# Retention: VectorE's routing work of an earlier group goes ahead of the residual and the keys

## The reference

```
x = x + attn(cond(x))                       # retention, 16 heads of 8
  attn: y = ((q k^T) * decay / sqrt(8)) v;  y = (y - mean) / sqrt(var + eps) per head
        return (y * gn_weight + gn_bias) @ W_o.T
x = x + ffn(cond2(x))
  cond2: gate = softmax(rmsnorm(x) @ wg_W + wg_b + cond_256 @ gg_W + gg_b)
         topk_w, topk_i = top_k(gate, 2);   only these two experts' outputs count
...                                         # second layer: field attention, delta rule, quaternions, ffn
```

## Time and profile before

| | us |
|---|---|
| three runs | 1911.68, 1920.77, 1924.03; median 1920.77 |
| the profiled execution, its own time | 1916.62 |
| its span in the trace | 1914.8 |
| mean granted TensorE clock over the span | 0.899 of full speed |
| busy: PE, DVE, ACT, POOL | 1644.5, 1256.0, 1082.9, 863.9 |

### The profile page before, as it was taken

One profiled execution on the slowest core, in us unless ns is written; L12 is line 12 of the kernel. 1 busy time (PEld: TensorE's weight loads), 2 busy tenths in 40 slices (PEclk: granted clock), 3 DMA queues, 4 the chain that ended last, 5 costly groups with the idle time before them and its releaser, 6 DMA issues. The chain is left out here.

```text
span 1914.8 us, 42986 instructions
## 1 busy us (share of the span) xinstructions
PE 1644.5 (86%) x15415; PEld 1172.7 (61%) x15415; DVE 1256.0 (66%) x3295; ACT 1082.9 (57%) x3196; POOL 863.9 (45%) x1080
## 2 busy tenths in 40 slices
PE   3788719994359966999998899999999999899988
PEld 0354418993359953656557777777777777566633
DVE  7587634554634556778765867777777777467767
ACT  2443204441124424879864667777777777767753
POOL 0235664664746631424323976707062534542223
PEclk8786759996579976999979999999999999999999
DMA  2940014323122243000003322122212132211001
GB/s 69 376 149 24 26 41 122 109 75 108 62 65 71 72 144 100 24 27 27 17 21 84 99 63 65 52 64 65 73 40 73 45 82 56 71 54 34 29 12 44
DMA packets 157665, 135.73 MB, mean 71 GB/s; under 512 B 90021, under 2 KB 130278, under 8 KB 155302
## 3 DMA queue, kind: packets, MB, share of 16 engines
q1 hardware_dynamic: 146950, 113.91, 20.2%
q0 software_dynamic: 9088, 18.70, 3.0%
q10 hardware_dynamic: 1440, 0.66, 0.1%
HBM read 76.65 MB, written 56.54 MB: 70 GB/s over the span
## 5 line engine op out<-in xcount | busy, mean ns | idle before, releaser
L849 POOL DMA_INDIRECT y<-moe_y,moe_aim x156 | 177.0, 1135 | 142.0 <-DVE moe_y L989 62.3
L2876 DVE TENSOR_TENSOR delta_sv<-delta_sv,delta_zp 32x256 f32<-32x256 f32 x384 | 161.3, 420 | 113.3 <-PE delta_zp L2442 105.6
L1811 ACT ACTIVATE field_p<-field_sp,field_nm 128x128 f32<-128x128 f32 x512 | 180.3, 408 | 7.2 <-DVE field_nm L1902 6.7
L2789 POOL TENSOR_TENSOR delta_dd<-delta_dd,delta_prod 128x30 f32<-128x30 f32 (+11 forms) x270 | 163.0, 604 | 21.2
L2787 POOL TENSOR_TENSOR delta_prod<-delta_ll,delta_dd 128x30 f32<-128x30 f32 (+11 forms) x270 | 143.9, 533 | 21.2
L2782 POOL TENSOR_TENSOR delta_dd<-delta_ll,delta_minus 128x1024 f32<-128x1024 f32 (+1 forms) x9 | 23.8, 2639 | 268.2 <-DMA delta_ll<-lanes 268.2
L1811 ACT ACTIVATION_READ_ACCUMULATOR field_p<-field_sp,field_nm 128x1 f32 x512 | 127.0, 248 | 0.0
L2442 PE MATMUL delta_zp<-delta_sv,delta_ct 128*32 128x128 f32 x1536 | 121.1, 279 | 4.8 <-DVE delta_sv L2876 4.4
L2860 DVE SCALAR_TENSOR_TENSOR delta_la<-delta_xp,delta_ck,delta_dc 128x256 f32<-128x256 f32 x256 | 107.5, 476 | 3.3 <-PE delta_xp L2400 1.5
L1912 DVE COPY field_pT<-field_ptp 128x512 f32<-128x512 f32 x128 | 84.1, 672 | 38.3 <-PE field_ptp L1661 38.3
L2442 PEld LDWEIGHTS delta_zp<-delta_sv,delta_ct 128*32 128x32 f32 x1536 | 69.6, 109 | 56.1 <-issue 24.7
(11 more groups left out here) (574 smaller groups left out, 4478.7 us busy)
## 6 DMA issues: line engine op xcount, KB each, us to landing
delta_al<-alpha SPq DMA_DIRECT2D x33, 512.0 KB, 4.4
pairs<-c_none SPq DMA_DIRECT2D x16, 1032.0 KB, 17.0
moe_xg<-pairs SPq DMA_DIRECT2D x78, 129.0 KB, 2.2
moe_yt<-y SPq DMA_DIRECT2D x16, 512.0 KB, 4.4
w_E<-in_E_dram SPq DMA_DIRECT2D x1, 4624.0 KB, 36.2
w_E<-in_E_dram SPq DMA_DIRECT2D x8, 578.0 KB, 4.1
lanes<-delta_la SPq DMA_DIRECT2D x256, 16.0 KB, 1.6
delta_di<-inverses SPq DMA_DIRECT2D x64, 64.0 KB, 2.4
```

The lines of the kernel that those rows point to most:

```text
L849: nc.gpsimd.indirect_dma_start(results, bass.IndirectOffsetOnAxis(ap=aim[:, t % AR, j:j + 1], axis=0), y[:, t % YS, j, :], None).then_inc( ...
L1811: last = nc.scalar.activation(p[:, slot, h, :], s_ps[i][:, k, :], ACT.Exp, bias=nm[:, slot, h:h + 1], accum_out=zs[:, slot, h:h + 1])
L2789: last = nc.gpsimd.tensor_tensor(dd[lanes, a + 1:, 0:a], dd[lanes, a + 1:, 0:a], pr, ALU.subtract)
L2876: nc.vector.tensor_tensor(sv[rows, two, :], sv[rows, two, :], z_ps[2 * pair // HH][rows, at, :], ALU.subtract).then_inc(s["z_kept"], 1)
```

## The change

In VectorE's loop, and nowhere else, `gate_place` of rounds 3 to 7 and `gate_pick` of rounds 2 to 6 move from behind `keep_k` to ahead of `residual`. In round 7 there is no `keep_k`, `gate_place` moves ahead of the residual and `gate_pick` stays behind it. Rounds 8 and 9 are as they were. No instruction is added, removed or altered.

```diff
                     if more:
                         keep_q(u + 1)
-                    if u == GROUPS:
+                    if 3 <= u <= GROUPS:
                         gate_place(nc, dve, ch, g, c, u - 3, seen[:, 64:64 + 2 * GB * NE])
+                    if more and 0 <= u - 2:
+                        gate_pick(nc, dve, ch, g, c, u - 2)
                     if normed:
                         residual(n)
                     if more:
                         keep_k(u + 1, 1 - half)
-                    if 0 <= u - 3 < GROUPS - 3:
-                        gate_place(nc, dve, ch, g, c, u - 3, seen[:, 64:64 + 2 * GB * NE])
-                    if 0 <= u - 2:
+                    if not more and 0 <= u - 2:
                         gate_pick(nc, dve, ch, g, c, u - 2)
                     if more:
                         decay(u + 1, 0)
```

## The result

The changed kernel took 1915.71 us (median of 20 runs, 1904.43 to 1922.87), the kernel before 1921.43 (20 runs, 1911.68 to 1934.84). The ratio is 0.9966 with a 95% interval of 0.9950 to 0.9981: 6.5 us faster, 3.7 to 9.6. The forecast was 6.0 us, to 1915.

What follows compares the result with a forecast made beforehand. VectorE was taken to bound fast rounds and TensorE, mostly at half clock, slow ones. Terms of -2.8 us at unchanged clocks and -3.2 for the clock gave -6.0, from 1920.77 to 1915 us; range 1904 to 1928.

Steps and rivals of the forecast that it cites:

- round 3 at half clock: Sign in the new profile that would show the forecast wrong: TensorE's clock at half in round 3; no size given.
- Fast rounds lose: Rounds 2 and 3: pick, or places and pick, delay the residual; +0.3 us and +0.95 us.
- The decay's wait goes in slow rounds: Ends of rounds 4 to 6: TensorE's wait for VectorE's decay falls from 2.4 to 4.0 us to about 1.
- The mask catches the moved work: Rounds 4 to 6: GpSimd's mask holds an instruction of places or pick; round 4 gains 1.06 us instead of 1.36.
- Rounds 4 to 6: Gains at unchanged clocks: 1.06 us in round 4, 1.06 in round 5, 1.5 in round 6.
- clock term: Round 5 begins at 2.4 GHz because TensorE's waits at round 4's end get shorter; -3.2 us, bounds 0 and -9.4.
- one for one: What rounds 2 to 6 gain or lose moves GpSimd's root at 217.71 and the stage's end by the same amount.
- 0.45 us more in round 7: Round 7: places run in the 4.03 us hole ahead of the residual, so GpSimd's scatter waits less; -0.45 us.
- Rival 4: Nothing reaches the stage's end, since GpSimd's scatters take up all that is won; 1920.8 us, chance 0.08.
- Rival 1: Only the waits change and the clock falls in round 5 as before; 1917 to 1918 us, chance 0.23.
- Rival 2: The clock stays up, rounds 4 and 5 take 18.4 to 20 us; 1903 to 1909 us, chance 0.15.
- Rival 3: Slower: late residual in fast rounds drops the clock a round earlier; 1927.5 us, up to 1937, chance 0.14.

Runs made afterwards that it cites:

- late_rounds: The changed kernel with the move kept in rounds 4 to 7 only, rounds 2 and 3 as before; 1913.81 us, ratio 0.9966 to the kernel before.
- early_rounds: The changed kernel with the move kept in rounds 2 and 3 only, rounds 4 to 7 as before; 1923.08 us, ratio 1.0016 to the kernel before.
- after_again: The changed kernel, unaltered, run and profiled a second time; ratio 0.9983 against the runs of the kernel before on its chip.
- before_again: The kernel before, unaltered, profiled a second time; rounds 4 to 6 together took 78.65 us.
- before_third: The kernel before, unaltered, profiled a third time; rounds 4 to 6 together took 78.49 us.
- before_filled: The kernel before plus two unread extra matmuls in TensorE's wait for the decay, at the start of rounds 4 to 7; 1916.47 us, ratio 0.9976.
- after_third: The changed kernel, unaltered, profiled a third time; rounds 4 to 6 together took 63.58 us.
- places_only: The changed kernel with only the places ahead of the residual, the pick back behind the keys; 1912.37 us, ratio 0.9942 to the kernel before.
- after_filled: The changed kernel plus two unread extra matmuls ahead of TensorE's transposes in rounds 3 to 6; 1918.11 us, ratio 0.9982 to the kernel before.
- places_filled: The kernel of places_only plus one unread extra matmul ahead of the scores at the start of rounds 3 to 7; 1912.11 us, ratio 0.9951.
- places_again: The same kernel as places_only, run again beside the changed kernel on one chip; 1911.70 us, ratio 0.9956 to the kernel before.

## Why the prediction was right, and where its terms were off

The direction and the order of size rest on the right mechanism: gate work ahead of the residual costs in fast rounds and pays in slow ones, and late_rounds and early_rounds show that the gain sits in the late ones. That the total came so near (-6.0 forecast, -6.5 measured) is in part luck: several terms were off, in opposite directions, and the second comparison gave only about half of it (0.9983). A sign that the prediction had named as "wrong", round 3 at half clock, stood at round 3's end in the first profile of the changed kernel and for over half of round 3 in after_again.

- *Fast rounds lose.* Right in sign, too small: +1.25 forecast for rounds 2 and 3, +4.2 on the mean of three profiles (+2.8 to +6.5). The sum had TensorE's scores at 1.14 us behind the new wait of some 2.2 us. The wait was 2.35, and the scores behind it ran 2.09 us: the clock was at half behind the new wait too, right where its next scores are on the path. I had argued that round 3's end, with more idle time and not less, made no difference to the clock; in the changed kernel's three profiles round 3 itself took 20.4 to 24.6 us.
- *The decay's wait goes in slow rounds.* Right, and by more than forecast: from 2.38 and 3.98 us to 0.23 and 0.19, where I had about 1.
- *The mask catches the moved work.* It did so in rounds 5 and 6, on the pick's last instruction, for about 0.6 us (3.84 and 3.85 instead of 3.26), and not in round 4, where I gave 1.2 to the places' last one. No instruction of the places or the pick took over 1 us in rounds 4 to 6, as I had expected of one. And I took the old place to be free of masks after a look at round 4 of one profile. It was caught in round 6 of that same profile, in rounds 4 to 6 of before_again and in 4 and 5 of before_third, for 1.6 to 1.8 us a round, and for 2.2 in before_filled's round 4. So the collisions spoke for this change more than against it.
- *Rounds 4 to 6.* -6.8 forecast with the clock term, -11.2 measured. By round, on the means of three profiles: round 4 -4.1 (forecast -1.06), round 5 -4.1 (forecast -1.06 and -3.2), round 6 -3.0 (forecast -1.5). Round 5 came out as forecast; round 4 is where the sum missed most. I had written that it stays slow, and it ran at 0.78, 0.78 and 0.99 instead of 0.63 to 0.75. Round 5 ran at 0.86, 0.78 and 0.94 instead of 0.64 to 0.76. How the gain of a round divides between the position, the collisions and the clock is not shown. At a clock near 1.00 round 4 took 23.14 us in before_filled and 19.02 in after_third, so at that clock the order alone, collisions included, may be worth 4.1 us, against the 1.1 to 1.4 that I gave it in a slow round; that is one profile against one, and before_filled holds two extra matmuls in its wait.
- *The premise of the clock term.* I set 1.01 us of waiting, which left the clock alone, against 1.90 and 2.38, which did not. The same profile of before holds a counter-example that I passed over: at the end of round 5 TensorE waited 2.44 us (ahead of 189.00), and the scores behind it ran 1.14 us, at full clock; the clock fell only some 2 us later. And places_only's round 2 and after_filled's round 4 ran slow behind waits of 1.04 us. No length of wait tells the two cases apart in these traces.
- *What passes to the stage's end.* I had "one for one", and 0.45 us more in round 7. The scatter's wait fell from 0.75 to 0.30 us, as forecast (the 0.3 us between two scatters is not in the earlier trace rows, but the trace has it). Yet on the mean 1.2 us were given back: in the first pair of profiles the root came 7.3 us earlier and the first load only 5.1. The reason is not shown: TensorE's waits for GpSimd's masks in round 7 add up to 3.9 to 4.0 us in the changed kernel's profiles, and to 2.6, 2.6 and 4.7 in those of before. Rival 4 is at most a small part of the truth.
- *Rival 1* is out, since the clock of rounds 4 and 5 changed as well as the waits. *Rival 2* came about in one execution: after_third's rounds 4 and 5 took 19.02 and 21.57 us at 0.99 and 0.94, and its single run was 7 to 9 us under the two of before taken beside it (1901.16 against 1908.51 and 1910.17). *Rival 3's* mechanism is there (after_again's round 3, the 22.50 us of early_rounds' round 3), but takes only some 4 of the 11 us that rounds 4 to 6 gain.

Open: why the residual of round 4 began at 155.14, 2.10 us behind a pick that had ended and an output that the trace ends at 152.99. Its releaser is given as "remote"; after_again and places_only have the same in round 4 (2.23 and 1.99 us), after_third, with TensorE at full clock there, has no such wait. And the whole program's time hides part of what a shorter retention gives: places_filled ended the stage 5.5 us before places_again and was no faster in the runs.

## What to carry to other kernels

Work that goes ahead of an instruction on which another engine waits is free only where that instruction was waiting itself; cost the move in each kind of round, and split it by size: here the 1.9 us piece belonged ahead of the residual and the 1.4 us piece into the gap that the next scores leave. A wait of 2 us on TensorE could cost twice here, once as itself and once as the half clock behind it, so ask of every moved wait what runs directly behind it. Read every round, and more than one profile, before calling a place free of collisions: a faster round moves the neighbour. And take no rule on the clock from one trace: look first in the same trace for a wait of the same length behind which the clock stayed up.

## What the runs showed of the hardware

- A single small VectorE instruction (32 elements a partition, about 0.2 us) took 1.14 to 1.99 us when a GpSimd multiply of 128x512 from SBUF ran beside it from near its start, and ended within 0.1 us of it: the scan L161 1.37 and 1.50 us, the addition L780 1.99, the `tensor_scalar` L140 1.14 to 1.16. Instructions that read PSUM kept their time beside the masks: the decay 1.87 to 1.89 us, the residual 0.68 to 0.69. So did the pick's L138 (0.16 us each from 177.65 on, under the mask of 177.64): most of the pick ran through that mask, only its last instruction did not.
- TensorE at half clock did not come back soon when it was busy: in round 5 of before_filled it was busy for all of the 20.0 us from 157 to 177, at a granted clock of 0.50; over the whole round it was busy 27.48 of 27.93 us at a mean of 0.63. In rounds 4 to 6 of the changed kernel's three profiles the mean clock of a round was 0.78 to 0.99, in those of before 0.63 to 0.83.
- A wait's length did not tell whether the clock would fall: 1.04 us ahead of round 2 was followed by a round at 1.00 in the three profiles of before and by one at 0.76 in places_only.
